# Attention and feed-forward block: single operations on their own slots, a reordered start, strided up-weight rows

## The chip, the cores and the metric

One core of a Trainium2 chip. The metric is the device time of one launch in microseconds (us), lower is better. The core has five engines that each run their own instruction stream in order and meet at semaphores: TensorE (PE, with its weight loads as PEld), VectorE (DVE), ScalarE (ACT), GpSimd (POOL) and SyncE (SP), which here issues nearly all transfers.

## What is computed

x is 16 batches of 128 x 512, the context 16 of 128 x 128. Per batch, with all weights shared:

```
x = x + xattn(layernorm(x), ctx, ctx)      # 16 query heads, 4 key/value heads of 32, rms norm,
                                           # rotary, causal softmax, out @ w_out.T
h = relu(layernorm(x) @ w_up.T + b_up + layernorm(x) @ A_up @ B_up)      # 512 -> 2048
x = x + h @ w_down.T + b_down + h @ A_down @ B_down                      # 2048 -> 512
w_up   = (w_up_q   - 7.5) * repeat(w_up_scale,   64)   # 4-bit values held in int32, 2048 x 512
w_down = (w_down_q - 7.5) * repeat(w_down_scale, 64)   # 512 x 2048
```

The kernel keeps near-float32 accuracy by splitting each fp16 operand into a high and a low part and multiplying three terms (high x high, high x low, low x high).

## The kernel before

**Weights.** The 2048 x 512 up weights and 512 x 2048 down weights arrive as eight groups of 1 MB in a staging ring of three (`load_group`, L269 to L273, SP). A group holds four tiles; there are 32 tiles. A tile is dequantised in place (even tiles on VectorE, L901; odd ones on GpSimd in two steps, L361 and L364), then TensorE adds the low-rank term (L683) and four 128 x 128 transposes (L638) into a 512-column PSUM bank, ScalarE copies out the high half (L500), TensorE subtracts that from the bank with a matmul against minus the identity (`weights_rest`, L698), and ScalarE copies out the low half (L505). Two banks, ff0 and ff1, serve these tiles and the feed-forward of all batches; a bank's next user waits for its last reader.

**Batches.** Each batch runs through: statistics, centring (L514), rotary products, splits of q and k, transposes by DMA (L304, L318), scores (L720), mask and row maximum (L999), exponentials (L543), reciprocal of the sums (L911), normalising on GpSimd (L387), high and low parts of the probabilities (L574, L396), four transposes by DMA (L326), the product with v (L735), its split (L532, L1020), the output projection (L748), residual (L978), second norm and its DMA transpose (L311), four up groups (L767), hidden activations (L930, L605, L939), four down parts (L782) and the result (L1045), which is stored by L277.

**Order.** There is no dynamic scheduler. All engines walk the same counter s (`for s in range(SLOTS)`); each stage has a constant R_... that says at which s batch 0 runs it and at which s batch 1 does, and from there each batch follows PERIOD = 8 slots later. Inside one slot an engine's operations follow the fixed order of its loop body, and each waits on its semaphores in place, so what stands behind a waiting instruction on the same engine waits too. A slot covers many instructions: with 8 slots to a batch, one is about an eighth of a batch's time. On TensorE the scores of a batch stand at slots 11 to 14, the product with v at 20, the projection at 22, up groups at 27 to 30, down parts at 31 to 34 (R_SCORES, R_PV, R_PROJ, R_UP, R_DOWN, L30 to L38). The 32 tiles have slots of their own (TILE_AT, L44); tile and rest are laid down together, and a weight group of the ring is reloaded at the slot of the last tile that frees it. On SP a slot's transposes of k, second norm, q and probabilities come before its weight load (L300 to L331).

**Start.** SP issues batch 0, the two scale tables, the norm weights, weight group 0, six small low-rank loads, batch 1, group 1, w_out, group 2 and more. The quantisation of all scales needs the largest absolute value of seven small arrays (`find_tops`, L837 to L845), a spread over partitions through TensorE (`spread_tops`), and a chain of small operations (`find_scales`), before any tile can be finished. The up bias is loaded as 16 x 128 and transposed on TensorE.

Of the kernel before, what the change touches and what calls it, by code (L numbers as in the profile page):

```python
# [25 lines left out]
PERIOD = 8  # L26
R_STATS, R_CENTRE, R_SINES, R_COSINES, R_ROPE = (0, 1), (1, 2), (1, 3), (1, 4), (2, 6)
R_KSPLIT, R_KLOW = (1, 3), (1, 4)
R_QSPLIT, R_QLOW = (2, 7), (2, 8)
R_SCORES = ((4, 11), (5, 12), (6, 13), (7, 14))  # L30
R_MASK = ((5, 12), (6, 13), (7, 14), (8, 15))
R_EXP = ((6, 13), (7, 14), (8, 15), (9, 16))
R_PROBS = ((7, 14), (8, 15), (9, 16), (10, 17))

R_PSPLIT = ((8, 15), (9, 16), (10, 17), (11, 18))
R_VSUM, R_VSPLIT = (5, 12), (6, 14)
# [7 lines left out]
TILE_AT = tuple(2 + (3 * t) // 4 if t < UP_TILES else 14 + (t - 16) // 2 if t < 26 else t - 7 for t in range(TILES))  # L44
DEQ_LEAD = 4
DVE_TILES = tuple(range(0, TILES, 2))
WOUT_AT = 4
# [3 lines left out]
def build(nc, x, ctx, qw, kw, wo, wuq, wus, bu, wua, wub, wdq, wds, bd, wda, wdb,  # L51
# [12 lines left out]
    SLOTS = PERIOD * (B - 2) + R_RESULT[1] + 1  # L64

    def at(s, r, after=0):
        if s - after == r[0]:
            return 0
        n, rest = divmod(s - after - r[1], PERIOD)
        return n + 1 if rest == 0 and 0 <= n < B - 1 else None  # L70

    with ExitStack() as es:
# [64 lines left out]
        b_nat = sb("b_nat", [HC, P])  # L137
# [23 lines left out]
        ff = [bank("ff0"), bank("ff1")]  # L161
# [3 lines left out]
        vb = bank("vb")  # L165
# [17 lines left out]
        ident_cast, minus_cast, b_turned = sem("ident_cast"), sem("minus_cast"), sem("b_turned")  # L183
# [4 lines left out]
        w_turned, w_high, w_rest, w_low = sem("w_turned"), sem("w_high"), sem("w_rest"), sem("w_low")  # L188
# [20 lines left out]
        wuq_v = wuq.rearrange("(g j p) c -> g p j c", p=P, j=4)  # L209
# [11 lines left out]
        def tiles_at(s):  # L221
            return [t for t in range(TILES) if TILE_AT[t] == s]

        def tiles_to_dequantise(s):
            return [t for t in range(TILES) if max(TILE_AT[4 * (t // 4)] - DEQ_LEAD + t % 4, 1) == s]

# [4 lines left out]
        tile_bank, up_bank, down_bank, up_taken = {}, {}, {}, {}  # L231
        tile_free, up_free, down_free = {}, {}, {}
        freed_by = [None, None]
        taken, last_bank, down_holds = 0, 1, None
        for s in range(SLOTS):
            for t in tiles_at(s):
                last_bank = 1 - down_holds if down_holds is not None else 1 - last_bank
                tile_bank[t], tile_free[t] = last_bank, freed_by[last_bank]
                freed_by[last_bank] = (w_low, t + 1)
            for g in range(4):  # L240
                n = at(s, R_UP, g)
                if n is not None:
                    down_holds = None
                    last_bank = 1 - last_bank
                    up_bank[n, g], up_free[n, g] = last_bank, freed_by[last_bank]
                    taken += 1
                    up_taken[n, g] = taken
                    freed_by[last_bank] = (ff_read, taken)
            n = at(s, R_DOWN)
            if n is not None:  # L250
                last_bank = 1 - last_bank
                down_bank[n], down_free[n] = last_bank, freed_by[last_bank]
                freed_by[last_bank] = (down_read, n + 1)
                down_holds = last_bank
# [4 lines left out]
        def _(sp):  # L259
# [20 lines left out]
            sp.dma_start(s_up[:], wus.rearrange("(c p) b -> p c b", p=P)).then_inc(scales_in, 16)  # L280
            sp.dma_start(s_dn[:], wds.rearrange("(c p) b -> p c b", p=P)).then_inc(scales_in, 16)
# [15 lines left out]
            for s in range(SLOTS):  # L297
                n = at(s, R_KLOW)
# [6 lines left out]
                n = at(s, R_NORM2)  # L305
# [6 lines left out]
                n = at(s, R_QLOW)  # L312
# [6 lines left out]
                for m in range(NN):  # L319
                    n = at(s, R_PSPLIT[m])  # L320
# [6 lines left out]
                for g in range(W_RING, 8):  # L327
                    if TILE_AT[4 * (g - W_RING) + 3] == s:
                        load_group(g)
                n = at(s, R_RESULT)  # L330
                if n is not None:  # L331
                    store(n)
                n = at(s, R_X1, 1)
# [6 lines left out]
        def _(pool):  # L340
# [26 lines left out]
            def keys(n):  # L367
                c, p = n % RING, n % 2
                pool.wait_ge(kv_in[c], 16 * (n // RING + 1))
                kv = kvt[:, c, :]  # L370
                if n > 0:
                    pool.wait_ge(k_low, n)
                pool.tensor_tensor(k_cos[:], kv, cwk[:], ALU.mult).then_inc(k_parts, 1)
# [72 lines left out]
            for s in range(1, SLOTS):  # L446
                probabilities(s)
                cosines(s)
                for t in tiles_to_dequantise(s):
                    if t not in DVE_TILES:  # L450
                        dequant(t)
                n = at(s, R_STATS)
                if n is not None:
                    keys(n)
# [663 lines left out]
```

## Time and profile before

| | |
|---|---|
| median of 3 runs | 587.93 us (584.47 to 588.89) |
| profiled execution, its own time | 587.63 us |
| its span, first to last instruction | 585.8 us |
| mean granted TensorE clock | 0.929 of full |
| busy share PE / DVE / ACT / POOL | 84% / 58% / 54% / 51% |
| chain that ended last: PE, POOL, DMA, issue | 45%, 20%, 10%, 8% |
| first result instruction of batch 0, of batch 15 | 171.76 us, 582.58 us |

### The profile page before, as it was taken

Reading aid. Unit: us, or ns where it says so; the run is one execution under the profiler, and the core shown is the slowest. Engines: PE = TensorE matmul, PEld = TensorE weight load, DVE = VectorE, ACT = ScalarE, POOL = GpSimd, SP = SyncE. Lnnn points to the kernel's source line nnn. Section 1 sums busy time; section 2 is a strip of 40 time slices with the busy share of each in tenths; the row PEclk is TensorE's granted clock in tenths of the full one; section 3 lists DMA queues with packets and bytes.
Section 4 is the critical chain, followed back from the end, with each engine's and each line's share of the span. In section 5 each row is a group of like instructions: output and inputs, shape, how many; then the busy total and the mean of one; then the engine's idle time right before and its main releaser. Section 6 shows DMA issues by size and latency. Waiting matters only on the chain.

```text
span 585.8 us, 12700 instructions
## 1 busy us (share of the span) xinstructions
PE 490.9 (84%) x4744; PEld 343.0 (59%) x4744; DVE 342.3 (58%) x1042; ACT 315.9 (54%) x947; POOL 301.4 (51%) x320
## 2 busy tenths in 40 slices
PE   0267456679888999989999989899999898999997
PEld 0134122337547676667677676767585757586783
DVE  2873513344456777675767758576767676564531
ACT  1557636373565665747484837383847464654210
POOL 3492474483174838383847556556657473625100
PEclk9999555759999999998999999899999998999999
DMA  8930652081053527180817282735455444536010
GB/s 171 284 84 2 191 131 62 29 190 32 10 89 88 123 56 139 39 167 10 167 21 157 39 138 47 131 61 118 56 122 98 84 95 57 103 52 109 2 38 18
DMA packets 144253, 52.87 MB, mean 90 GB/s; under 512 B 132768, under 2 KB 135088, under 8 KB 144144
## 3 DMA queue, kind: packets, MB, share of 16 engines
q1 hardware_dynamic: 141344, 51.56, 43.3%
q10 hardware_dynamic: 2768, 0.34, 0.5%
q8 instruction: 37, 0.61, 0.4%
q14 instruction: 24, 0.20, 0.1%
q0 software_dynamic: 80, 0.16, 0.1%
HBM read 16.39 MB, written 4.19 MB: 35 GB/s over the span
## 4 chain that ended last, share of the span: by engine, by line
PE 45%; POOL 20%; DMA 10%; issue 8%; ACT 6%; DVE 6%; SPq 5%; POOLq 0%; ACTq 0%; DVEq 0%
PE ff L767 19%; PE ff L782 8%; DMA pT<-big 8%; PE tb L748 8%; POOL big L396 6%; POOL pr L387 5%; PE ff L638 3%; SPq L326 3%; POOL y L436 3%; PE tb L735 2%; ACT pr L543 2%; PE sb L720 1%; PE ff L683 1%; POOL inv L379 1%; DVE x L978 1%
## 5 line engine op out<-in xcount | busy, mean ns | idle before, releaser
L767 PE MATMUL ff<-xnT,wu_hi 128*128 128x128 f16 x2048 | 184.2, 223 | 2.7 <-DVE y L1045 1.2
L767 PE MATMUL ff<-xnT,wu_lo 128*128 128x128 f16 x1024 | 180.4, 223 | 0.0
L767 PEld LDWEIGHTS ff<-xnT,wu_hi 128*128 128x128 f16 x2048 | 162.3, 100 | 13.7 <-issue 7.4
L782 PE MATMUL ff<-wd_hi,x 128*128 128x512 f16 x512 | 152.4, 379 | 3.1 <-DVE z L930 2.3
L387 POOL TENSOR_TENSOR pr<-pr,rinv 128x512 f32<-128x512 f32 x64 | 74.5, 1164 | 137.3 <-DVE rinv L911 137.3
L605 ACT ACTIVATE x<-z 128x512 f16<-128x512 f32 x64 | 40.3, 630 | 119.5 <-DVE z L930 119.5
L767 PEld LDWEIGHTS ff<-xnT,wu_lo 128*128 128x128 f16 x1024 | 102.4, 100 | 0.0
L543 ACT ACTIVATE pr<-pr,nmax 128x128 f32<-128x128 f32 x256 | 98.7, 388 | 4.3 <-DVE nmax L999 4.3
L782 PE MATMUL ff<-wd_lo,x 128*128 128x512 f16 x256 | 97.0, 379 | 0.0
L782 PEld LDWEIGHTS ff<-wd_hi,x 128*128 128x128 f16 x512 | 48.8, 98 | 63.4 <-issue 4.9
L396 POOL TENSOR_TENSOR big<-pr,big 128x512 f16<-128x512 f32 x64 | 78.7, 1238 | 3.4 <-ACT big L574 3.4
L930 DVE SCALAR_TENSOR_TENSOR z<-ff,su,b_up 128x512 f32<-128x512 f32 x64 | 47.8, 747 | 46.1 <-PE ff L767 46.1
L999 DVE CUSTOM_DVE_ANT_0 pr<-sb,tabs,score_scale 128x128 f32<-128x128 f32 x256 | 74.2, 346 | 0.0
L939 DVE SCALAR_TENSOR_TENSOR x<-z,x 128x512 f16<-128x512 f32 x64 | 51.8, 809 | 5.0 <-ACT x L605 4.9
L543 ACT ACTIVATION_READ_ACCUMULATOR pr<-pr,nmax 128x1 f32 x256 | 48.2, 188 | 0.0
L574 ACT ACTIVATE big<-pr 128x512 f16<-128x512 f32 x64 | 39.5, 618 | 9.2 <-POOL pr L387 8.9
L782 PEld LDWEIGHTS ff<-wd_lo,x 128*128 128x128 f16 x256 | 25.0, 98 | 30.2
L911 DVE RECIPROCAL rinv<-scaled_sum 128x4 f32<-128x4 f32 x64 | 11.1, 173 | 53.5 <-ACT scaled_sum L548 53.2
L638 PE MATMUL ff<-tabs,big 128*128 128x128 f32 x128 | 30.1, 378 | 8.0 <-POOL big L364 8.0
L426 POOL TENSOR_TENSOR inv<-arg,minus_half 128x1 f32<-128x1 f32 x16 | 9.2, 572 | 50.3 <-DVE arg L985 50.3
L1045 DVE SCALAR_TENSOR_TENSOR y<-ff,sd,y 128x512 f32<-128x512 f32 x16 | 12.0, 751 | 39.3 <-PE ff L782 39.3
L735 PE MATMUL tb<-pT,v 128*32 128x512 f16 x192 | 14.3, 406 | 20.5 <-DMA pT<-big 20.5
(139 smaller groups left out, 716.0 us busy)
## 6 DMA issues: line engine op xcount, KB each, us to landing
xt<-in_x SPq DMA_DIRECT2D x16, 256.0 KB, 3.1
big<-in_L_ffn_w_up_q SPq DMA_DIRECT2D x4, 1024.0 KB, 11.8
big<-in_L_ffn_w_down_q SPq DMA_DIRECT2D x4, 1024.0 KB, 5.4
out<-y SPq DMA_DIRECT2D x16, 256.0 KB, 2.5
kvt<-in_ctx SPq DMA_DIRECT2D x16, 64.0 KB, 3.3
wd_lo<-in_L_xattn_w_out SPq DMA_DIRECT2D x1, 1024.0 KB, 14.1
pT<-big SPq DMA_TRANSPOSE x64, 3.4
wd_hi<-in_L_ffn_w_up_lora_b SPq DMA_DIRECT2D x3, 128.0 KB, 8.6
```

Source lines behind the costliest of these rows:

```text
L387: pool.tensor_tensor(pr[:, m], pr[:, m], rinv[:, p, 4 * m:4 * m + 4].unsqueeze(2).broadcast_to([P, NG, P]), ALU.mult).then_inc(probs, 1)
L396: pool.tensor_tensor(p3[:, m, :, 1, :], pr[:, m], p3[:, m, :, 0, :], ALU.subtract).then_inc(p_low, 1)
L543: last = act.activation(pr[:, m, g, :], pr[:, m, g, :], ACT.Exp, bias=nmax[:, p, j:j + 1], scale=-1.0, accum_out=rsum[:, p, j:j + 1])
L574: act.activation(p3[:, m, :, 0, :], pr[:, m], ACT.Copy).then_inc(p_high, 1)
L605: act.activation(x2_hi[:, HG * g:HG * g + HG, :], z[:, g % 2], ACT.Relu).then_inc(x2_high, 1)
L638: return pe.matmul(dst, src, ident[0:src.shape[0], 0:src.shape[0]], is_transpose=True, **kw)
L748: last = pe.matmul(tb[0][:], a[:, m, :], b[:, m, :], start=(i == 0 and m == 0), stop=(i == 2 and m == NN - 1))
L767: last = pe.matmul(bank[:, P * h:P * h + P], a[:, m, cols], b[:, m, :], start=(h == 0 and m == 0 and i == 0), stop=(m == KC - 1 and i == 2 ...
L782: last = pe.matmul(ff[down_bank[n]][:], a[:, h, :], b[:, h, :], start=(h == 0 and i == 0), stop=(h == HC - 1 and i == 2))
L930: dve.scalar_tensor_tensor(z[:, g % 2], ff[up_bank[n, g]][:].rearrange("p (h t) -> p h t", h=HG), su[:], b_up[:, HG * g:HG * g + HG].unsqu ...
L939: dve.scalar_tensor_tensor(x2_lo[:, HG * g:HG * g + HG, :], z[:, g % 2], 0.0, x2_hi[:, HG * g:HG * g + HG, :], ALU.max, ALU.subtract).then ...
L999: last = dve.tensor_tensor_reduce(pr[:, m, g, :], sbk[m % 2][:, P * g:P * g + P], mask, score_scale[:], 3e38, ALU.add, ALU.min, nmax[:, p, ...
```

## The change

Nothing of the arithmetic changes. What does:

1. **Slots.** PERIOD is 264 and every operation has a slot of its own for batches 0, 1, 2 and 3 (from 3 on, +264 each); tiles, their rests, copies and loads too. The loop bodies keep their fixed order only inside one (now very fine) slot.
2. **Banks.** Four ff banks instead of two. The bank vb goes; the column sum for v is now written into tb[0], the bank of the projection.
3. **Low halves of 15 tiles on VectorE.** For the tiles in LOW_BY_DVE one VectorE subtraction (bank minus high half) replaces TensorE's L698 and ScalarE's L505.
4. **w_out** is reordered on VectorE, not on ScalarE.
5. **Loads.** Up weights: a partition holds four neighbouring rows (8 KB in one piece instead of 4 x 2 KB); the up scales, the down low-rank factor and the up bias follow the same order, the bias in place without a transpose. The down tiles then read every fourth column of the staging buffer, and the up low-rank operand is read with a step of four. SP issues the norm weights first and waits for the five small loads before weight group 0. The up scales go out on ScalarE's queue.
6. **z buffer.** The hidden activations of a group wait for x2_low (VectorE) instead of x2_high (ScalarE) of two groups before.

```
-PERIOD = 8
-R_SCORES = ((4, 11), (5, 12), (6, 13), (7, 14))
-R_PV, R_OSPLIT, R_PROJ, R_X1, R_POW2, R_NORM2 = (13, 20), (14, 21), (14, 22), (15, 23), (15, 23), (16, 24)
-R_UP, R_DOWN = (18, 27), (22, 31)
-R_RESULT = (26, 35)
+PERIOD, FREE = 264, 3
+R_SCORES = ((290, 603, 1007, 1208), (295, 618, 1009, 1209), (349, 636, 1097, 1233), (383, 647, 1130, 1257))
+R_SUMS = ((330, 680, 1078, 1248), (347, 704, 1125, 1324), (368, 746, 1155, 1378), (402, 774, 1181, 1428))
+R_VSUM = (452, 492, 629, 1160)
+R_PV = (504, 903, 1238, 1544)
+R_PROJ = (529, 935, 1374, 1622)
+R_X1 = (570, 929, 1400, 1649)
+R_UP = ((712, 1182, 1498, 1790), (719, 1197, 1508, 1857), (753, 1211, 1518, 1914), (796, 1216, 1613, 1942))
+R_DOWN = ((881, 1228, 1633, 1963), (964, 1378, 1667, 1990), (1114, 1404, 1739, 2016), (1139, 1481, 1741, 2043))
+R_RESULT = (1140, 1487, 1789, 2048)
...
-TILE_AT = tuple(2 + (3 * t) // 4 if t < UP_TILES else 14 + (t - 16) // 2 if t < 26 else t - 7 for t in range(TILES))
+LOW_BY_DVE = (1, 4, 7, 10, 13, 15, 16, 18, 20, 22, 25, 27, 28, 30, 31)
+TURN_AT = (231, 275, 350, 423, 464, 496, 497, 498, 513, 548, 559, 590, 594, 616, 621, 642, 695, 706, 763, 831, 862, 863, 871,
+           904, 925, 955, 979, 984, 1011, 1033, 1045, 1102)
+LOAD_AT = (186, 582, 594, 641, 810)
...
-    def at(s, r, after=0):
-        if s - after == r[0]:
-            return 0
-        n, rest = divmod(s - after - r[1], PERIOD)
-        return n + 1 if rest == 0 and 0 <= n < B - 1 else None
+    def at(s, r):
+        if s in r[0:FREE]:
+            return r.index(s)
+        n, rest = divmod(s - r[FREE], PERIOD)
+        return n + FREE if rest == 0 and 0 <= n < B - FREE else None
...
-        ff = [bank("ff0"), bank("ff1")]
+        ff = [bank("ff0"), bank("ff1"), bank("ff2"), bank("ff3")]
-        vb = bank("vb")
...
-        wuq_v = wuq.rearrange("(g j p) c -> g p j c", p=P, j=4)
+        wuq_v = wuq.rearrange("(g p j) c -> g p j c", p=P, j=4)
...
             load_batch(0)
-            sp.dma_start(s_up[:], wus.rearrange("(c p) b -> p c b", p=P)).then_inc(scales_in, 16)
-            sp.dma_start(s_dn[:], wds.rearrange("(c p) b -> p c b", p=P)).then_inc(scales_in, 16)
             for src, dst in ((kw, kw_bc), (qw, qw_bc)):
...
-            load_group(0)
+            sp.dma_start(s_dn[:], wds.rearrange("(c p) b -> p c b", p=P)).then_inc(scales_in, 16)
             for i in range(3):
...
+            sp.wait_ge(scales_in, 16 * 5)
+            load_group(0)
+            load_group(1)
             load_batch(1)
-            load_group(1)
+            load_group(2)
             sp.dma_start(wo_raw, wo.rearrange("(j p) c -> p j c", p=P)).then_inc(wout_in, 16)
-            load_group(2)
...
                 for i in range(4):
-                    last = turn(bank[:, P * i:P * i + P], stage[:, g % W_RING, i, P * j:P * j + P],
+                    rows = slice(P * j, P * j + P) if t < UP_TILES else slice(j, None, 4)
+                    last = turn(bank[:, P * i:P * i + P], stage[:, g % W_RING, i, rows],
...
-                    pe.matmul(vb[:, 0:1], ones[:], ssq[:, n % 2:n % 2 + 1], start=True, stop=True).then_inc(v_summed, 1)
+                        if projs_before[n] > 0:
+                            pe.wait_ge(x1_ready, projs_before[n])
+                    pe.matmul(tb[0][:, 0:1], ones[:], ssq[:, n % 2:n % 2 + 1], start=True, stop=True).then_inc(v_summed, 1)
...
+            def weights_low(t):
+                dve.wait_ge(w_high, t + 1)
+                hi, lo = ((w[:, t % 4, 512 * (t // 4):512 * (t // 4) + 512] for w in (wu_hi, wu_lo)) if t < UP_TILES else
+                          (w[:, t - UP_TILES, :] for w in (wd_hi, wd_lo)))
+                dve.tensor_tensor(lo, ff[tile_bank[t]][:], hi, ALU.subtract).then_inc(w_low_v, 1)
```

On TensorE the order within one steady period, with the slot in the period, is now: up group 1 (9), projection (38), up group 2 (66), up group 3 (94), column sum for v (104), down part 0 (115), down part 1 (142), scores 0 and 1 of a later batch (152, 153), down part 2 (168), scores 2 (177), down part 3 (195), scores 3 (201), up group 0 of the next batch (206), product with v (224).

## Rows read from the trace of the kernel before

**Rows 1.** Stages: length, busy (x instructions) of PE, PEld, DVE, ACT, POOL; clock, DMA share, GB/s.
```profile
32.20:171.80 139.60, 98.04 (x549) 57.10 (x549) 60.28 (x178) 81.07 (x223) 71.97 (x76) 0.74 0.32 76
32.20:49.20 17.00, 14.74 (x53) 8.65 (x53) 11.45 (x19) 9.52 (x19) 12.04 (x12) 1.00 0.16 31
56.00:110.60 54.60, 29.85 (x104) 15.30 (x105) 18.57 (x64) 26.43 (x80) 28.48 (x32) 0.50 0.41 111
117.40:134.50 17.10, 13.05 (x62) 7.65 (x63) 6.36 (x10) 11.20 (x28) 14.86 (x16) 0.50 0.81 175
171.80:510.80 339.00, 317.06 (x3389) 231.27 (x3390) 233.77 (x730) 202.31 (x647) 199.85 (x205) 0.98 0.49 93
510.80:582.60 71.80, 71.74 (x785) 51.71 (x782) 30.90 (x79) 21.39 (x60) 15.99 (x16) 1.00 0.25 44
```

**Rows 2.** Timeline, VectorE, three of sixteen results: start, duration, instruction, idle before it.
```profile
171.76 0.74 DVE L1045 SCALAR_TENSOR_TENSOR y<-ff,sd,y 128x512 f32<-128x512 f32 x1
510.76 0.75 DVE L1045 SCALAR_TENSOR_TENSOR y<-ff,sd,y 128x512 f32<-128x512 f32 x1 [3.80 <-PE ff L782]
582.58 0.75 DVE L1045 SCALAR_TENSOR_TENSOR y<-ff,sd,y 128x512 f32<-128x512 f32 x1 [8.22 <-PE ff L782]
```

**Rows 3.** Chain that ended last, pieces of one late batch: start, duration, what.
```profile
497.50 2.86 PE tb L748 x12
500.35 10.38 PE ff L782 x48
510.73 2.68 PE ff L767 x48
513.41 0.23 PE sb L720 x4
513.63 0.17 PE vb L706 x2
516.73 0.76 PE tb L735 x12
```

**Rows 4.** Waits, 200 to 480 us: total us, times, longest us.
```profile
PE tb L735 <- DMA pT<-big: 15.9, 10, 2.4
```

**Rows 5.** Timeline of the opening, four instructions of the way to the first tile.
```profile
5.62 0.46 SPq L284 DMA_DIRECT2D wd_hi<-in_L_xattn_q_norm_w  x1
12.14 0.88 DVE L828 TENSOR_REDUCE wmax<-wd_hi 128x1 f32<-128x512 f32 x2 [7.02 <-DMA wd_hi<-in_L_xattn_q_norm_w]
30.73 1.35 POOL L364 TENSOR_TENSOR big<-big,s_up 128x512 f32<-128x512 f32 x1
32.23 1.08 PE L638 MATMUL ff<-tabs,big 128*128 128x128 f32 x4 [1.34 <-POOL big L364]
```

**Rows 6.** Timeline, TensorE: three long idle times while the weights are built.
```profile
69.28 0.61 PE L698 MATMUL ff<-wu_hi,minus 128*128 128x512 f16 x1 [6.01 <-ACT wu_hi L500]
80.06 1.09 PE L638 MATMUL ff<-tabs,big 128*128 128x128 f32 x4 [5.47 <-POOL big L364]
106.63 2.07 PE L748 MATMUL tb<-wo_hi,oT_hi 128*128 128x512 f32 x4 [8.95 <-DVE oT_lo L1020]
```

**Rows 7.** Timeline, SyncE's queue: loads of weight groups and a transpose before one.
```profile
57.32 1.19 SPq L304 DMA_TRANSPOSE kT<-k  x1
58.56 0.58 SPq L273 DMA_DIRECT2D big<-in_L_ffn_w_up_q  x1
99.01 0.57 SPq L273 DMA_DIRECT2D big<-in_L_ffn_w_down_q  x1
```

**Rows 8.** Timeline, VectorE: what waited for the later load.
```profile
104.14 0.69 DVE L901 SCALAR_TENSOR_TENSOR big<-big,s_dn 128x512 f32<-128x512 int32 x1 [8.08 <-DMA big<-in_L_ffn_w_down_q]
```

**Rows 9.** Busy time of line 698 alone while the weights are built (PE, PEld).
```profile
32.20:171.80 139.60, 17.25 (x32) 3.58 (x32) 0.74 0.32 76
```

**Rows 10.** Lines by form, 0 to 172 us: count, busy us, mean ns; idle before.
```profile
L638 PEld LDWEIGHTS ff<-tabs,big 128*128 128x128 f32 x128 | 19.3, 188 | 19.6 <-issue 19.6
L683 PE MATMUL ff<-wd_lo,a_up 48*128 48x512 f16 x16 | 9.2, 576 | 2.1 <-DVE wd_lo L890 2.1
```

More of the change, by code:

```diff
@@ L219, in scale_of, with low_of, wait_lows @@
             return v.unsqueeze(2).broadcast_to([P, 8, QB])
[L221 to L225, printed above, removed]
+        def low_of(t):
+            return (w_low_v, LOW_BY_DVE.index(t) + 1) if t in LOW_BY_DVE else (w_low, t + 1 - len([u for u in LOW_BY_DVE if u < t]))
+        def wait_lows(eng, last):
+            by_dve = len([u for u in LOW_BY_DVE if u <= last])
+            if by_dve <= last:
+                eng.wait_ge(w_low, last + 1 - by_dve)
+            if by_dve:
+                eng.wait_ge(w_low_v, by_dve)
@@ L227, in build @@
         b_pieces = ((b_up3[:, 0:512], b_up_in[:, 0:512], 4), (b_up3[:, 512:], b_up_in[:, 512:], 4),
                     (b_dn3[:], b_dn_in, 5))
[L231 to L234, printed above, removed]
-        for s in range(SLOTS):
[L236 to L239, printed above, removed]
+        tile_bank, up_bank, down_bank, tile_free, up_free, down_free = {}, {}, {}, {}, {}, {}
@@ new lines, in build, with next_bank @@
+        freed_by, last_bank, down_holds = [None] * 4, 3, None
+        def next_bank():
+            b = (last_bank + 1) % 4
+            return (b + 1) % 4 if b == down_holds else b
+        projs_before, sums_before = {}, {}
+        for s in range(SLOTS):
+            n = at(s, R_VSUM)
+            if n is not None:
+                projs_before[n] = len(sums_before)
+            n = at(s, R_PROJ)
+            if n is not None:
+                sums_before[n] = len(projs_before)
+        for s in range(SLOTS):
+            for t in range(TILES):
+                if TURN_AT[t] == s:
+                    last_bank = t % 4 if t < UP_TILES else 2 + t % 2
+                    tile_bank[t], tile_free[t] = last_bank, freed_by[last_bank]
+                    freed_by[last_bank] = low_of(t)
@@ L256, in build @@
+                n = at(s, R_DOWN[g])
+                if n is not None and g == 0:
+                    last_bank = down_holds = 0 if n == 0 else next_bank()
+                    down_bank[n], down_free[n] = last_bank, freed_by[last_bank]
+                    freed_by[last_bank] = (down_read, n + 1)
+                if n is not None and g == 3:
+                    down_holds = None
         block = es.enter_context(nc.Block())
@@ L445, in _ @@
             pool.wait_ge(v_powers_set, 2)
-            for s in range(1, SLOTS):
+            for s in range(SLOTS):
                 probabilities(s)
                 cosines(s)
-                for t in tiles_to_dequantise(s):
-                    if t not in DVE_TILES:
+                for t in range(TILES):
+                    if DEQ_AT[t] == s and t not in DVE_TILES:
                         dequant(t)
-                n = at(s, R_STATS)
+                n = at(s, R_KEYS)
+                if n:
+                    keys(n)
+                n = at(s, R_POW)
                 if n is not None:
-                    keys(n)
+                    norm_factors(n)
                 norm_and_residual(s)
@@ L693, in weights_rest @@
             def weights_rest(t):
-                if t == 0:
+                if t == min(u for u in range(TILES) if u not in LOW_BY_DVE):
                     pe.wait_ge(minus_cast, 1)
@@ L785, in feed_forward @@
                             last.then_inc(down_done, 1)
+            pe.wait_ge(consts_in, 16)
+            spread_tops()
             for s in range(SLOTS):
                 turns(s)
[L789 to L802 removed]
+                for i in range(3):
+                    if LORA_TURN_AT[i] == s:
+                        lora_turn(i)
+                for t in range(TILES):
+                    if REST_AT[t] == s and t not in LOW_BY_DVE:
+                        weights_rest(t)
+                    if TURN_AT[t] == s:
+                        weights(t)
+                for m in range(NN):
+                    if WO_TURN_AT[m] == s:
+                        wout_turn(m)
                 feed_forward(s)
[L804 to L805 removed]
                 products(s)
```

363 lines of the change are left out of this document (197 added, 166 removed).

## The prediction, made before the changed kernel was run

> **What bounds the kernel now.** The stage table comes first, because the busy shares of the whole span mix two stages [rows 1]. From 32.2 to 171.8 us the weights are built: TensorE is busy 98.04 of 139.6 us, and no other engine reaches 82. From 171.8 to 510.8 us only batches run and TensorE is busy 317.06 of 339.0; from 510.8 to 582.6 it has no gap left (71.74 of 71.8). So TensorE is the bound in the second and third stage, and waits are in the first. 
>
> The results of the batches give the rate [rows 2]: 510.76 - 171.76 = 339.0 us for twelve intervals, 28.25 us each. The chain that ended last shows what one batch costs TensorE at the upper level [rows 3]: four up groups of 2.68, the down product 10.38, projection 2.86, product with v 0.76, four scores of 0.23 and the column sum 0.17, together 25.81 us. Twelve are 309.7 us. The other 29.3 us of that stage are 7.4 of longer instructions (317.06 - 309.7, among them those in short stretches of lower clock; the mean is 0.98) and 21.9 of idle time. The waits name it: the product with v waited for the last DMA transpose of the probabilities ten times, 15.9 us, 2.4 at most [rows 4], which makes 19.1 in twelve batches.
>
> **The change, part by part.** I split the profiled execution (587.63 us) into the time to the first result 171.8, twelve intervals 339.0, the last three 71.8, and 5.05 from the last result to the end.
>
> *Opening.* The first tile's transposes began at 32.23, waiting for GpSimd's second multiplication (30.73, 1.35 us) [rows 5]. The norm weights, issued at 5.62, held VectorE until 12.14; now they are issued right behind batch 0, and ScalarE centres batch 0 before its low-rank work, which lets GpSimd's first tiles start earlier. Group 0 is issued later than now, since SP waits for the five small loads, so it becomes the second thing that could be last. The first tile stands at slot 231; if a slot is a tenth of a us (264 of them would be 26.4 us, just over the 25.81 of work) that is 23 us. I take 24, so -8, between 0 (group 0's landing takes back all that was gained) and -9.
>
> *Low halves.* Line 698 cost TensorE 17.25 us for 32 tiles [rows 9]; 15 go: -8.1. VectorE gains 15 subtractions out of PSUM, at the 0.75 us of its nearest form, the result instruction [rows 2], 11 us, beside its 60.28 of 139.6 busy [rows 1]: cost nothing, as that engine has 79 us free; without this cover it would be those 11. Moving w_out's reordering from ScalarE to VectorE, and dropping the bias transpose, I take as nothing for the same reason.
>
> *Idle time in this stage.* It is 139.6 - 98.04 = 41.6 us. Three gaps hold 6.01 + 5.47 + 8.95 = 20.4 of it [rows 6], and I trace all three to weight loads issued late. SP issued the load of group 3 at 58.56, directly behind a transpose of k that itself had to wait (57.32) [rows 7]; a later load went out only at 99.01, VectorE stood 8.08 us in a dequantisation that needed it [rows 8], and the small subtraction that the projection needed was queued behind it on VectorE, so TensorE stood 8.95 us in the projection with finished tiles behind it. In the new order the load of group 3 stands before every transpose of probabilities and of batch 1, and the others right at the tiles that free their buffer; on VectorE the dequantisations stand behind the work of batch 0 that TensorE waits for. With four banks, a tile whose copy is late also no longer stops the next but one. I take the 20.4 as gone and 21.2 as staying; bounds: none goes, or all but 10.
>
> *Clock.* TensorE did 14.74 + 29.85 + 13.05 = 57.6 us of work at its lower level in this stage [rows 1]; at the upper one it would be half. A denser stage should spend less time there, but I can't show how much: between 0 and -25 I take -7, nearer to nothing, as the engine was 87% busy from 32.2 to 49.2 and stayed at the lower level until then.
>
> First result: 171.8 - 8 - 8.1 - 20.4 - 7 = 128.3 us.
>
> *Steady state.* Work stays at 25.81 plus 0.61 of longer instructions. From scores 3 to the product with v there were 6 of 8 slots, 0.75 of 28.25 = 21.2 us; now there are 287 of 264, 1.09 periods or 29 us. Eight us more room against waits of at most 2.4 should end that wait. What is late next is, I think, nothing of that size, but in-order engines always leave something: I take 0.4 of idle time for the 1.83 now, 26.8 us per batch. Bounds: 26.4 (no idle) and 28.25 (all comes back). Twelve: 321.6. The slots of the first results stand 347 and 302 apart, not 264: 121 slots, 0.46 of a period, 12 us, because the attention of batches 1 and 2 was kept back for the weights. I take half, +6, between 0 and 12. The last three stay at 71.8 and the end at 5.05.
>
> Sum: 128.3 + 6 + 321.6 + 71.8 + 5.05 = 532.7, **533 us**. The profiled execution stands 0.3 us under the median of 587.93, which I leave out.
>
> **The strides.** The 64 transposes of down tiles now load every fourth column of a float32 buffer, and the up low-rank operand is read with a step of four. No row shows TensorE reading with a step. The nearest are the plain forms, 188 ns for a float32 weight load and 576 ns for the low-rank matmul [rows 10]. If either took twice as long, it would be 64 x 0.188 = 12.0 and 16 x 0.576 = 9.2 us; below nothing there is no reason for a gain. I take 0, since the loads run beside other matmuls, and carry 21 us as a rival.
> The Trainium skill, "SBUF — State Buffer", section "Door 1: The DMA port swizzle", speaks against this part: accesses that stay within a 16-byte line run at full bandwidth and each one that crosses to a new line pays, so that a step of four float32 is at the edge. By that rule the down tiles would pay (an estimate by it, with the row's 188 ns: 545 us) and the fp16 operand, with a step of 8 bytes, would not. No row of this trace can say.
>
> **The rivals.**
> - *The steady waits come back* at another place: 12 x (28.25 - 26.8) = 17.4 more, 550 us. For it: four engines above 50% busy in one fixed order. Against: only one place waits now. 0.12.
> - *The weight stage keeps its 27 us* of idle time and low clock, since group loads and dequantisation are what they were: 533 + 27.4 = 560. For it: the load ring is still three groups. Against: the late issues are visible in rows. 0.12.
> - *The strides cost*: 533 + 21 = 554. 0.08.
> - *Slower: the shared bank.* The column sum for v now goes into tb[0], so TensorE stops there (slot 104) until VectorE's residual of the same batch (65) has read it, with all four down parts queued behind. That residual stands behind the reciprocal of sums 2 (58), which waits for ScalarE's exponentials (56). A late exponential thus stops TensorE, which it can't do now. Slack by the slots: 39 of 264, 4 us. It would turn the sign from (587.6 - 532.7) / 12 = 4.6 us of standstill per batch; with 6 it gives 533 + 72 = 605. 0.07.
> - *Nothing gained*: the waits of both stages all re-form and pay for the shorter opening, 588 us. 0.05.
>
> My forecast has 0.56. The range takes in its bounds and the three milder rivals: low, first result 117 (all but 10 us of the idle time gone, clock as taken), no delay of the first intervals, 26.5 per batch, 117 + 318 + 71.8 + 5.05 = 512, I say 513; high, first result 150, 12 us of delay, 28.25 per batch, 578, I say 576. Within 1% is what a measurement of this kernel can't tell from no change. Faster by over 1%: forecast and first three rivals, 0.88; within 1%: 0.05; slower: 0.07.
>
> **What would show it.** First transposes of a tile at 23 to 26 us; no VectorE wait for a down load above 3 us; first result near 128; thereafter 26.4 to 27.3 us between results, with no wait of the product with v for its transpose; the column sum with no idle time before it (or, if the rival holds, some us in each batch, released by VectorE's residual); float32 weight loads of down tiles at 188 ns. The forecast is wrong if the first result comes after 150, or if intervals stay over 28.

## The result

The changed kernel takes 516.28 us (median of four, 516.16 to 516.8) against 587.44 beside it: ratio 0.8796, 95% interval 0.8761 to 0.8831, 12% faster. The same kernel in a later comparison gave 516.6 against 588.83, 0.8785 (0.8759 to 0.881). The profiled execution took 516.16 us, with a span of 514.4.

The page of the changed kernel, its first lines, the granted clock and the chain that ended last:

```profile
span 514.4 us, 12676 instructions
...
PE 471.2 (92%) x4728; PEld 335.4 (65%) x4728; DVE 353.7 (69%) x1061; ACT 302.4 (59%) x928; POOL 293.0 (57%) x320
...
PEclk9996797899999999999999999999999999999999
...
PE 83%; DVE 5%; DMA 4%; POOL 2%; SPq 2%; issue 2%; ACT 1%; POOLq 0%
```

The chain is TensorE for 83% (45% before) and GpSimd for 2% (20% before). The stages, in the columns of [rows 1]:

```profile
27.40:125.30 97.90, 84.41 (x536) 54.30 (x536) 69.54 (x195) 70.68 (x198) 64.02 (x67) 0.86 0.42 105
27.40:38.00 10.60, 9.71 (x44) 6.49 (x44) 9.79 (x44) 8.69 (x36) 7.94 (x10) 1.00 0.23 50
...
41.40:58.50 17.10, 13.78 (x54) 7.59 (x53) 12.18 (x18) 11.22 (x21) 12.99 (x13) 0.50 0.50 118
...
75.60:82.40 6.80, 5.14 (x49) 5.14 (x50) 0.18 (x1) 6.00 (x25) 5.33 (x6) 0.50 0.16 32
...
96.10:99.50 3.40, 3.21 (x10) 1.60 (x11) 2.82 (x6) 2.44 (x5) 1.45 (x3) 0.51 1.14 295
...
155.10:440.20 285.10, 285.10 (x3110) 207.74 (x3107) 213.48 (x677) 183.30 (x600) 174.19 (x187) 1.00 0.54 100
440.20:511.10 70.90, 70.87 (x771) 50.89 (x768) 28.15 (x60) 17.04 (x41) 13.84 (x14) 1.00 0.15 35
```

The row to look at is 155.10 to 440.20: TensorE is busy 285.10 of 285.10 us, so it waits for no other engine and no transfer, at a granted clock of 1.00.
```profile
125.28 0.75 DVE L1133 SCALAR_TENSOR_TENSOR y<-ff,sd,y 128x512 f32<-128x512 f32 x1 [0.97 <-PE ff L861]
```
```profile
440.18 0.75 DVE L1133 SCALAR_TENSOR_TENSOR y<-ff,sd,y 128x512 f32<-128x512 f32 x1 [2.33 <-PE ff L861]
```
```profile
511.11 0.75 DVE L1133 SCALAR_TENSOR_TENSOR y<-ff,sd,y 128x512 f32<-128x512 f32 x1 [8.22 <-PE ff L861]
```

Split as the prediction split it, in us of the two profiled executions:

| | before | forecast | after | gained |
|---|---|---|---|---|
| to the first result | 171.8 | 128.3 | 125.3 | 46.5 |
| twelve intervals | 339.0 | 327.6 | 314.9 | 24.1 |
| last three | 71.8 | 71.8 | 70.9 | 0.9 |
| to the end | 5.05 | 5.05 | 5.05 | 0 |
| sum | 587.6 | 532.7 | 516.2 | 71.5 |

### The profile page after: what moved, and what is told of

The parts are those of the page before. It is cut to its first block, busy times and chain, and to the rows that moved or that the text cites. A ratio compares the mean times of both kernels' runs of the same rounds, so it can differ in the third digit from the quotient of the medians.

```text
span 514.4 us, 12676 instructions
## 1 busy us (share of the span) xinstructions
PE 471.2 (92%) x4728; PEld 335.4 (65%) x4728; DVE 353.7 (69%) x1061; ACT 302.4 (59%) x928; POOL 293.0 (57%) x320
## 4 chain that ended last, share of the span: by engine, by line
PE 83%; DVE 5%; DMA 4%; POOL 2%; SPq 2%; issue 2%; ACT 1%; POOLq 0%
PE ff L846 32%; PE ff L861 30%; PE tb L826 8%; PE ff L710 4%; PE sb L799 2%; PE tb L814 2%; PE ff L757 2%; DMA wd_hi<-in_L_xattn_q_norm_w 1%; SPq L395 1%; DMA xnT<-xn_parts 1%; DVE big L977 1%; POOL big L469 1%; DMA qT<-q 1%; ACT pr L616 1%; DVE wd_lo L966 1%
## 5 line engine op out<-in xcount | busy, mean ns | idle before, releaser
L846 PE MATMUL ff<-xnT,wu_hi 128*128 128x128 f16 x2048 | 178.9, 221 | 3.8 <-DMA xnT<-xn_parts 2.9
L846 PE MATMUL ff<-xnT,wu_lo 128*128 128x128 f16 x1024 | 176.0, 220 | 0.0
L846 PEld LDWEIGHTS ff<-xnT,wu_hi 128*128 128x128 f16 x2048 | 158.1, 99 | 13.4 <-issue 9.7
L460 POOL TENSOR_TENSOR pr<-pr,rinv 128x512 f32<-128x512 f32 x64 | 68.3, 1070 | 61.1 <-DVE rinv L999 61.0
L846 PEld LDWEIGHTS ff<-xnT,wu_lo 128*128 128x128 f16 x1024 | 101.0, 99 | 0.0
L1027 DVE SCALAR_TENSOR_TENSOR x<-z,x 128x512 f16<-128x512 f32 x64 | 56.9, 891 | 0.7 <-ACT x L678 0.6
L492 POOL TENSOR_TENSOR t_cos<-xc,cw 128x512 f32<-128x512 f32 x16 | 25.8, 1611 | 18.4 <-ACT xc L587 18.3
L605 ACT ACTIVATE oT_hi<-tb,v_scales 128x512 fp32r<-128x512 f32 x16 | 11.0, 688 | 40.5 <-PE tb L814 40.5
L710 PE MATMUL ff<-tabs,big 128*128 128x128 f32 x128 | 27.0, 343 | 0.2 <-DVE big L977 0.2
L799 PEld LDWEIGHTS sb<-kT,qT 96*128 96x128 f16 x256 | 18.7, 101 | 10.9 <-DVE nmax L1087 1.1
```

Source lines behind the costliest of these rows:

```text
L460: pool.tensor_tensor(pr[:, m], pr[:, m], rinv[:, p, 4 * m:4 * m + 4].unsqueeze(2).broadcast_to([P, NG, P]), ALU.mult).then_inc(probs, 1)
L710: return pe.matmul(dst, src, ident[0:src.shape[0], 0:src.shape[0]], is_transpose=True, **kw)
L846: last = pe.matmul(bank[:, P * h:P * h + P], a[:, m, cols], b[:, m, :], start=(h == 0 and m == 0 and i == 0), stop=(m == KC - 1 and i == 2 ...
L1027: dve.scalar_tensor_tensor(x2_lo[:, HG * g:HG * g + HG, :], z[:, g % 2], 0.0, x2_hi[:, HG * g:HG * g + HG, :], ALU.max, ALU.subtract).then ...
```

## The experiments

Two theories stand against each other. **Waits**: the 71 us are standstills of in-order engines that the new places of the operations take away. **Work**: part of it is cheaper work and transfers (low halves off TensorE, wider pieces of the weight loads, the held-back start). The runs that change one place of the order test the first, the others the second.

### One number for one operation: the product with v 60 slots earlier

```
-R_PV = (504, 903, 1238, 1544)
+R_PV = (504, 903, 1238, 1484)
```

> The changed kernel with the product with v 60 slots earlier from batch 3 on (1484 instead of 1544; it moves in front of the last two down parts and two score groups of the batch before), nothing else. The room from the last scores to it falls from 287 to 227 of 264 slots, from 28 to 22 us; the kernel before had 21.2. Theory 'room': the wait for the transpose is back, 1 to 4 us in each of 12 batches, intervals of 27 to 30 us instead of 25.9, 530 to 560 us. Rival 'the fine order shortened the way of the probabilities itself': no wait and 516 to 518.

588.74 us, ratio 1.0005 (0.9975 to 1.0036): 72 us more than the changed kernel, by the place of one group of twelve matmuls from batch 3 on. The wait came back, as expected; the price is far above the expected 530 to 560 us, which counted only the wait itself. The first result, then the waits of this run from 200 to 480 us, then a stage of it:

```profile
126.48 0.75 DVE L1133 SCALAR_TENSOR_TENSOR y<-ff,sd,y 128x512 f32<-128x512 f32 x1 [0.99 <-PE ff L861]
```

```profile
PE tb L814 <- DMA pT<-big: 34.1, 9, 4.1
```

```profile
250.80:254.20 3.40, 3.40 (x18) 1.06 (x11) 0.00 (x0) 3.26 (x10) 1.23 (x2) 0.50 0.00 0
254.20:281.50 27.30, 24.05 (x266) 18.04 (x263) 18.62 (x60) 12.61 (x43) 14.52 (x16) 1.00 0.51 95
281.50:284.90 3.40, 2.92 (x16) 0.88 (x17) 0.19 (x3) 3.37 (x13) 1.04 (x1) 0.50 0.02 5
```

TensorE waits 34.1 us in nine batches, 3.8 each, for the probabilities' last transpose, more than twice what it was before the change [rows 4]. Most intervals are 31.4 us, which is also above the 28.25 of the kernel before: the first result keeps its gain of 45 us, and the steady stage loses more than the change had given it. And the clock falls: 3.4 us at 0.50 (6.8 in four of twelve batches), 27.3 us at 1.00, and again. In the changed kernel it doesn't fall in the 415 us from 99.5 to the end. So a wait costs more than its length: 3.8 us of waiting and some 1.7 us for each stretch at 0.50 (3.4 us of work at half rate) make the 5.5 us by which most intervals grew.

The timelines also show that the way of the probabilities did not get shorter. From the last scores of a batch (on TensorE, L720 before, L799 after) to the last of four transposes on SyncE's queue, before and after:

```profile
325.67 0.39 PE L720 MATMUL sb<-kT,qT 96*128 96x128 f16 x4
```
```profile
341.76 2.76 SPq L326 DMA_TRANSPOSE pT<-big  x2
```
```profile
258.63 0.39 PE L799 MATMUL sb<-kT,qT 96*128 96x128 f16 x4
```
```profile
278.56 2.61 SPq L395 DMA_TRANSPOSE pT<-big  x2
```
```profile
287.53 0.83 PE L814 MATMUL tb<-pT,v 128*32 128x512 f16 x12
```

Both rows of the queue hold the last two transposes. From the scores' row to the end of the issue it is 18.9 us before and 22.5 after; what changed is that the product with v comes 28.9 us after the scores' row. The other batches of the two traces agree (18.7 to 19.6 us and 22.5 to 22.8). The wait ended because its consumer was put later, not because the work in front of it became faster.

### The same move in the coarse order

Three kernels were made from the one before. The first moves the product with v and what follows up to the second norm, the last one moves the feed-forward and the result too:

```
-... = (13, 20), (14, 21), (14, 22), (15, 23), (15, 23), (16, 24)      # b6, b7 and b8
+... = (13, 21), (14, 22), (14, 23), (15, 24), (15, 24), (16, 25)
-R_UP, R_DOWN = (18, 27), (22, 31)                                     # b8 only
+R_UP, R_DOWN = (18, 28), (22, 32)
-R_RESULT = (26, 35)
+R_RESULT = (26, 36)
```

> The kernel before with the product with v, its split, the projection, the residual and the second norm one slot of eight later from batch 1 on. Theory 'room': the wait for the last transpose of the probabilities (1.6 us per batch) goes, intervals fall from 28.25 to 26.4 to 26.9, 12 x 1.5 = 16 to 20 us less, 568 to 572. Rival 'another wait takes its place': the up groups now follow the second norm's transpose by two slots instead of three and TensorE waits there; intervals stay above 27.5 and the time above 580.

620.22 us, ratio 1.0533 (1.0484 to 1.0583). The rival is right: the wait for the probabilities is gone, and this one stands in its place (waits from 200 to 480 us), with intervals of 30.4:

```profile
PE ff L767 <- DMA xnT<-xn_parts: 29.7, 10, 3.8
```

> The kernel before with everything from the product with v to the result one slot later from batch 1 on, so that only the room between the probabilities' last transpose and the product with v grows (6 to 7 of 8 slots) and the distance from the second norm to the up groups stays. Theory 'two rooms are needed': both waits are absent, intervals of 26.0 to 26.8 us instead of 28.25, 12 x 1.7 = 20 us less, 565 to 573. Rival 'the coarse order itself costs': the wait appears in a third place and intervals stay above 27.5, 580 or more.

580.49 us, ratio 0.9865 (0.9828 to 0.9902): the rival's time, but not by a wait in a third place. Intervals fall from 28.25 to 27.5, and the old wait is smaller but there:

```profile
PE tb L735 <- DMA pT<-big: 12.1, 10, 2.3
```

With a whole slot more room the way of the probabilities itself, measured as above, took 20.1 to 21.6 us to the end of its last transpose instead of 18.7 to 19.6, presumably since VectorE, ScalarE and GpSimd now have other work at the same slots. A slot of eight is 3.5 us; the waits to be removed are 1.6. I found no whole-slot move that fits, and that is what single slots repair; that none exists isn't shown.

> Both moves in the kernel before. If the two places are independent, the gains add: 548 to 560 us. What then is left to the changed kernel's 516 is the opening (5 us), the low halves (4 to 8), the clock and the finer order. Rival: one gain hides the other and the sum falls short by more than 5 us.

614.06 us, ratio 1.0437 (1.0393 to 1.0481): b6's move plus the one below, and nowhere near the expected 548 to 560. It is 6 us under b6's move alone, about the 5 us that the one below gains alone, so the two places do add, on top of a wrong move.

### Weight loads

```
             for s in range(SLOTS):                     # SyncE's loop of the kernel before
+                for g in range(W_RING, 8):
+                    if TILE_AT[4 * (g - W_RING) + 3] == s:
+                        load_group(g)
                 n = at(s, R_KLOW)
...
-                for g in range(W_RING, 8):
-                    if TILE_AT[4 * (g - W_RING) + 3] == s:
-                        load_group(g)
```

> The kernel before with one move: in each slot SyncE issues the weight group's load ahead of the slot's transposes. Theory 'loads stuck behind transposes' (the idle-time step of the prediction): group 3 goes out at about 46 us instead of 58.56 and group 5 some us before 99, the waits of 6.0, 5.5 and 9.0 us on TensorE shrink: 10 to 20 us less, 568 to 578. Rival 'the engines' order is the trouble, not the queue': GpSimd and VectorE stand in other waits at the same places and the time falls by less than 4 us.

582.95 us, ratio 0.9896 (0.9847 to 0.9944); first result at 164.8 instead of 171.8. SyncE's queue, and TensorE's longest wait:

```profile
40.53 0.39 SPq L273 DMA_DIRECT2D big<-in_L_ffn_w_up_q  x1
```
```profile
91.10 1.19 SPq L307 DMA_TRANSPOSE kT<-k  x1
92.34 0.57 SPq L273 DMA_DIRECT2D big<-in_L_ffn_w_down_q  x1
```
```profile
100.08 1.22 PE L748 MATMUL tb<-wo_hi,oT_hi 128*128 128x512 f32 x2 [9.07 <-DVE oT_lo L1020]
```

Between the theory and the rival: 5.3 us by the medians, 7 by the first result. Group 3 goes out 18 us earlier; the gap of 6.0 us is gone, the one of 5.5 is 3.2. The load of group 5 also went out 11 us earlier (71.01 instead of 82.38), behind these gaps. The later load, that of group 6 and not of group 5 as expected above, is as late as before, now behind a transpose of an earlier slot (91.10), 9 us after the last tile that frees its buffer (that tile began at 81.3), and the wait of 9.07 us stays with it. So the prediction's cause holds for group 3; for the later load this kernel did not remove it, and whether an earlier load alone would end the 9 us stays open.

```
-LOAD_AT = (186, 582, 594, 641, 810)
+LOAD_AT = (495, 582, 594, 641, 810)
```

> The changed kernel with one number altered: SyncE issues weight group 3 behind the four transposes of batch 0's probabilities (slot 495 instead of 186), so at about 49 us instead of 37.45. Theory 'late loads stop in-order engines': the data lands near 55, VectorE stands in the dequantisation of tile 12 meanwhile with the low half of tile 4 behind it, which frees the bank of tile 8, so TensorE stands 4 to 7 us around 50 to 57: 520 to 524 us, first result 4 to 8 us later. Rival 'the load has slack': group 3 is turned only at 65, 16 us after 49, and the time stays within 1 us of 516.3.

518.12 us (514.86 to 519.11), ratio 0.8798 (0.8745 to 0.8852): not to be told from the changed kernel. The load did go out late:

```profile
50.44 0.57 SPq L342 DMA_DIRECT2D big<-in_L_ffn_w_up_q  x1
```

It was 37.45. The first half of the expected chain came: VectorE stood in the dequantisation of tile 12 until 56.25 for this load. The second didn't:

```profile
56.25 0.69 DVE L977 SCALAR_TENSOR_TENSOR big<-big,s_up 128x512 f32<-128x512 int32 x1 [3.92 <-DMA big<-in_L_ffn_w_up_q]
```

VectorE had stood 2.5 us three operations later in the changed kernel too, for ScalarE's high half of tile 7, so most of the 3.92 replaced that, and TensorE lost 0.20 us there. Tile 12 began at 65.0 in the changed kernel, well behind 56. The late wait found work in front of it that was late anyway: slack, here.

### Low halves

```
-LOW_BY_DVE = (1, 4, 7, 10, 13, 15, 16, 18, 20, 22, 25, 27, 28, 30, 31)
+LOW_BY_DVE = (1, 25, 28)
```

with slots for the 12 tiles' matmul and copy between their high half and the bank's next user.

> The changed kernel with the low halves of 12 of the 15 tiles given back to TensorE (matmul against minus the identity) and ScalarE; tiles 1, 25 and 28 stay on VectorE. Theory 'TensorE is the bound while the weights are built': 12 more matmuls of 0.22 to 0.54 us on TensorE and 12 copies of 0.59 on ScalarE, plus the hops between them: 4 to 8 us more, 520 to 524. Rival 'there was room': TensorE still stands 13.5 us in that stage and they fall into it, 516 to 517.

544.46 us, ratio 0.9257 (0.9204 to 0.931): 28 us more, first result at 151.1. The direction is that of the first theory, the size three and a half to seven times what it gave. Its stage, and the longest of its stretches at 0.50, which last 17.1, 27.3, 10.2 and 10.2 us here against 17.1, 6.8 and 3.4 above:

```profile
27.50:151.10 123.60, 99.84 (x549) 60.00 (x548) 64.75 (x183) 77.93 (x215) 67.23 (x67) 0.74 0.34 83
...
65.60:92.90 27.30, 23.10 (x110) 14.89 (x111) 10.31 (x45) 14.23 (x41) 14.57 (x18) 0.50 0.39 111
```

TensorE is busy 15.4 us longer (99.84 against 84.41) and stands 10.3 us longer (23.8 against 13.5). Twelve matmuls at 0.6 us are 7.2 us at most; the rest of the busy time goes, I think, with the low clock. The low half on TensorE is a round trip, ScalarE to TensorE to ScalarE, in front of the bank's next user, and one subtraction on VectorE is not. A reservation: the twelve slots were mine, put into an order laid out without them; a new layout for them might cost less than 28.

### Strided reads

```
-rows = slice(P * j, P * j + P) if t < UP_TILES else slice(j, None, 4)
+rows = slice(P * j, P * j + P)
-..., b_up3[:, 512 * g:512 * g + 512].rearrange("k (p i) -> k i p", i=4)
+..., b_up3[:, 512 * g:512 * g + 512]
```

> The changed kernel with plain reads: TensorE's transposes of down tiles read 128 neighbouring columns instead of every fourth, and the up low-rank operand is read without a step. This mixes up the order of the hidden units between the two weight matrices, so the products belong to other rows; nothing else changes, and every instruction stays in its place. Theory 'the step costs': in the changed kernel's trace the low-rank matmul of an up tile takes 607 ns at the granted clock 1.0 where the plain one of a down tile takes 386, and a float32 weight load of a down tile 196 to 220 ns where that of an up tile takes 140. Some nine up tiles and all down tiles lie at the upper clock, TensorE is nearly always busy there, so 9 x 0.22 + 16 x 0.09 = 3.4 us go: 513 us, with 386 ns and 140 ns in the rows. Rival 'the step is hidden': 516.3, with the same rows or with the time turned into waits.

516.53 us (515.32 to 517.87), ratio 0.8786 (0.8748 to 0.8825): no difference. But the prices are real. Lines by form where the clock is at 1.00: the changed kernel's up tiles (59 to 71 us; weight loads of the transposes and low-rank matmuls) and its down tiles (84 to 125; of this 3.4 us are at 0.50, and from 99.6 on alone the mean is 209 ns too), then the down tiles with plain reads (84 to 100):

```profile
L710 PEld LDWEIGHTS ff<-tabs,big 128*128 128x128 f32 x28 | 2.9, 141 | 3.1 <-issue 3.1
...
L757 PE MATMUL ff<-wd_lo,a_up 48*128 48x512 f16 x7 | 4.2, 607 | 0.0
```
```profile
L710 PEld LDWEIGHTS ff<-tabs,big 128*128 128x128 f32 x56 | 8.0, 209 | 3.4 <-issue 3.4
```
```profile
L710 PEld LDWEIGHTS ff<-tabs,big 128*128 128x128 f32 x20 | 2.1, 140 | 1.1 <-issue 1.1
```

A float32 weight load takes 209 ns with a step of 16 bytes and 140 without; the fp16 operand takes 607 ns with a step of 8 bytes, and in the plain run 387. The 3.4 us that this is worth on TensorE did not reach the end; with plain reads the stretches of low clock lay elsewhere (6.8 us twice). The Trainium skill, "SBUF — State Buffer", section "Door 1: The DMA port swizzle", has every access that crosses to a new 16-byte line pay, and steps within a line free: this trace agrees for the float32 load (209 ns against 140) and not for the fp16 operand, whose step of 8 bytes should be free by it (607 ns against 387).

### The held-back start

```
-            sp.wait_ge(scales_in, 16 * 5)
             load_group(0)
```

> The changed kernel without SyncE's wait for the five small loads ahead of weight group 0. Theory 'the hold pays': group 0 goes out at about 7.1 us instead of 11.07, shares the transfer engines with the scales and the bias, these land 2 to 3 us later, the search for the largest values starts that much later and so does the first tile: 518 to 519 us. Rival 'order is enough': the small loads are all issued by 3.4 us, well ahead of 7.1, so the norm weights and scales land as now (the reductions start at 11.9 +- 0.5) and the time stays at 516.3 or falls by at most 1, since group 0 is not what the first tile waits for.

517.47 us (514.65 to 519.42), ratio 0.8798 (0.8751 to 0.8845): nothing. The search for the largest values began at 12.38 us instead of 11.91 and the first tile's transposes at 27.8 instead of 27.4. The hold neither pays nor costs that can be seen; the small loads are ahead of group 0 in the queue in both kernels.

### The clock of the first stage

```
+            def warm(k, bank=ff[3]):
+                for _ in range(k):
+                    pe.matmul(bank[:], ident16[:], ident16[:].unsqueeze(1).broadcast_to([P, 4, P]), ...)
+            warm(22)                 # ahead of the largest values; 26 behind, 9 behind the low-rank transposes
...
+                    pe.wait_ge(row_max, 3)           # e10 only: third and fourth transposes of w_out
+                    warm(12 if m == 2 else 4, sbk[0])
...
+                        warm(9, sbk[0])              # e10 only: ahead of the column sum of batch 0
...
+                                pe.wait_ge(row_max, 7)
+                                warm(13, sbk[0])     # e10 only: ahead of up group 0 of batch 0
```

> The changed kernel again, unaltered, as the base for what runs beside it on the same chip. Both theories: 514.5 to 519 us; the spread of the small experiments before (514.7 to 519.4) is then that of the kernel itself, and differences below 2 us between them say nothing.

516.6 us (516.4 to 517.22), the base of the next two. Its first result comes at 126.23 us. From 27.4 us on its trace has two stretches at 0.50 on record, of 6.8 and 3.4 us; before the first change on record, at 56, its float32 transposes take 1.12 us for four, so it was at the lower level there as well.

> The changed kernel with 57 matmuls of no use (identity by identity, 128 x 512 fp16, into a bank that is free until its first tile) in TensorE's idle times of the opening: 22 before the search for the largest values, 26 behind it, 9 behind the low-rank transposes. Theory 'the clock costs': TensorE is at 2.4 GHz when the first tile comes at 27.4 us instead of 38.0; 9.7 us of work up to 38 run at twice the rate, but the softmax of batch 0 on ScalarE and VectorE sets the end there, so 2 to 5 us less. Rival 'TensorE's clock in the opening is covered': within 1 us of the base, or slower by up to 3 if the extra matmuls come in the way of the small ones.

519.68 us (519.22 to 520.73), ratio 0.8838 (0.8812 to 0.8864), 3 us slower than its base, so the rival, at its worse end. The clock was at 1.00 from 9.9 us, but the way to the first tile is VectorE's and its transposes began 0.4 us earlier only; then the clock fell at 30.4 and again at 40.6, where TensorE stands. Up to 78 us the two traces agree within 0.3. The first results lie 2.2 us apart (128.41 and 126.23), and the product with v of batch 1 shows where that begins, here and in the base:

```profile
103.23 0.83 PE L814 MATMUL tb<-pT,v 128*32 128x512 f16 x12 [3.12 <-DMA pT<-big]
```
```profile
102.64 0.83 PE L814 MATMUL tb<-pT,v 128*32 128x512 f16 x12 [0.20 <-DMA pT<-big]
```

TensorE is there 2.3 us earlier than in the base, stands 3.12 us for the last transpose, and starts 0.6 us later; the other 1.6 us come behind it, where a stretch at 0.50 lies at 105.5 to 108.9, and in the base in front of it (97.0 to 100.4). Why the transpose came later no run shows.

> As the kernel with 57 matmuls of no use, and 38 more where TensorE waits while the weights are built: 12 and 4 ahead of the third and fourth transposes of w_out, 9 ahead of the column sum of batch 0, 13 ahead of up group 0 of batch 0, into the score bank that is free there. Theory 'idle gaps take the clock down and the low clock prolongs the stage': the stretches at 0.5 (41.4 to 58.5, 75.6 to 82.4, 96.1 to 99.5, 27.3 us with 22.1 us of work in them) shrink or go, up to 11 us less together with the opening, first result at 114 to 120, 505 to 512 us. Rival 'other engines hold the stage': the clock rises and the time stays within 2 us of the base.

511.07 us (509.48 to 513.13), ratio 0.8691 (0.8664 to 0.8717) against the base's 0.8785 (0.8759 to 0.881): 5.5 us faster than the changed kernel and 8.6 faster than with the opening's matmuls alone, the fastest of all. TensorE, then the stage:

```profile
36.82 2.75 PE L874 MATMUL sb<-ident 128*128 128x512 f16 x12
```
```profile
27.40:120.80 93.40, 83.10 (x574) 50.85 (x573) 71.99 (x194) 70.39 (x197) 66.20 (x67) 0.96 0.46 110
32.60:36.00 3.40, 3.40 (x16) 2.27 (x16) 3.14 (x22) 3.34 (x19) 1.62 (x2) 0.50 0.01 2
36.00:97.40 61.40, 54.36 (x428) 33.67 (x427) 47.43 (x100) 45.91 (x120) 50.79 (x49) 1.00 0.59 145
97.40:100.90 3.50, 3.50 (x12) 2.44 (x12) 3.02 (x7) 3.09 (x8) 1.70 (x3) 0.51 0.61 119
```

The stretches at 0.50 after 27.4 us shrink from the 27.3 us on record in the changed kernel's first trace to 6.8, and the first result comes at 120.9 instead of 126.2. The first theory had the mechanism right, the price about half: it allowed 11 us and 5.5 came, because in these stretches ScalarE and VectorE are as busy as TensorE (11.22 and 12.18 of 17.10 us against 13.78) and then hold the stage, I think.

## Why the prediction was right, step by step

The time lies in the range and faster was right; the forecast of 533 was 17 us too high. The steps hold in kind, with one reservation: that late loads caused the idle time is shown for a part of it only. These are the terms.

*Opening*, 8 us forecast, 4.8 measured (32.23 to 27.44). The changed kernel, four instructions of the way:

```profile
11.07 0.82 SPq L342 DMA_DIRECT2D big<-in_L_ffn_w_up_q  x2
...
15.98 0.62 POOL L430 TENSOR_SCALAR big<-big 128x512 f32<-128x512 int32 x1 [0.34 <-DMA big<-in_L_ffn_w_up_q]
...
26.66 0.61 PE L757 MATMUL ff<-wd_lo,a_up 48*128 48x512 f16 x1 [2.13 <-DVE wd_lo L966]
...
27.44 0.90 PE L710 MATMUL ff<-tabs,big 128*128 128x128 f32 x3 [0.17 <-DVE big L977]
```

Group 0 was not last: its data were in at 15.98. The norm weights came 3.4 us earlier and this went through, but VectorE's own chain of small operations, and its low-rank subtraction that the first tile's low-rank matmul waits for, now set the first tile.

*Low halves and clock*, 8.1 and 7 forecast: TensorE's busy time from the first tile to the first result fell by 13.6 us (98.04 to 84.41), 15.1 by the sum. Work done at the lower level fell from 57.6 us to 31.8 (9.71 + 13.78 + 5.14 + 3.21 in the stages above), which at half rate is 12.9 us, nearly twice my 7. This and the 8.1 overlap, as low halves that left had been done at the lower level, and the strided reads took some back. That the low halves are worth more than their matmuls, I had not seen: experiment, 28 us for twelve.

*Idle time*, 41.6 us, 21.2 forecast to stay; 13.5 stayed. The gap of 8.95 us in the projection is gone, those that are left are 2.9 and less. Two of the longest:

```profile
41.13 0.88 PE L710 MATMUL tb<-tabs,x 128*128 128x128 f32 x4 [2.91 <-DVE wo_lo L971]
```
```profile
77.26 0.40 PE L846 MATMUL ff<-xnT,wu_hi 128*128 128x128 f16 x2 [2.93 <-DMA xnT<-xn_parts]
```

The direction and the places were right. That the late loads were the cause is shown for group 3 only (7 us of 12 for its two gaps).

*Steady state*, 26.8 forecast, 25.91 measured. Here two sub-terms were mis-sized. I left 0.4 us of idle time and there is none. And I kept 0.61 us per batch of "longer instructions" as if they were work: most of it was the stretches of low clock (three of 3.4 us at half rate are 5.1 of the 7.4 us), and these went with the waits; 0.1 stayed. Twelve times 0.89 are 10.7 of the 17 us. 25.81 from [rows 3] was the number to trust. The first intervals cost 4.0 us more than 25.9, 6 forecast; the last three 70.9, 71.8 forecast.

*Strides*, 0 forecast with 21 as the rival: the operations do cost more (1.5 and 1.6 times), the kernel doesn't.

*Rivals.* The shared bank never stopped TensorE: between 155.1 and 440.2 us there is no idle time at all ahead of anything, the column sum included, so its 4 us of slack by the slots were enough. That waits come back at another place did not happen, but the two moved kernels show that it easily does: 28.25 became 30.4 by the move that ended the wait I had named.

Of the 71 us, then, the two traces place 46 before the first result and 24 in the twelve intervals. The experiments price parts of the new order, not shares of the 71: the low halves of twelve tiles are worth 28 us in it, and the place of one consumer 72, which is three times what the steady stage had gained, because the misplaced product makes the intervals longer than they were before the change. Such prices overlap and don't add up to a budget. Not tried alone are the early norm weights, the wider pieces of the weight loads, w_out on VectorE, the new wait for the z buffer and the four banks; as for the banks, in the new order the low half of a tile stands behind the turns of later tiles, so I expect two to lock it.

## What to carry to other kernels

When engines run in order and one of them is nearly full, read for each of its waits two numbers: how long the way of the data is, and how far behind its producer the consumer stands; put the consumer past the end of the way (here 28.9 us behind its producer for a way of 22.5), and check the next consumer down the line, because the wait moves there (one group 60 of 264 slots too early cost 72 us, one slot of eight too late cost 32). Count time above an engine's bare work as waiting until shown otherwise, its slower clock included. Slots of 3.5 us could not remove waits of 1.6 here; single ones of 0.1 us did.

## What the runs showed of the hardware

- The granted clock also falls where TensorE's waits are short. With 3.8 us of standstill per batch of 31 us it is at 0.50 for 3.4 or 6.8 us in nearly every batch; with 1.6 us per batch of 28 us three times in 339 us; in the changed kernel, with 1.3 us from 99.5 to 125.3, 2.8 us to 155.1 and none after that, never.
- From 41.4 to 58.5 us it stayed at 0.50 with TensorE 81% busy, 7.30 of its 13.78 busy us in float32 transposes. Why it didn't rise sooner no run shows. With matmuls of no use in the idle times (2.75 us of them from 36.82 on, two groups more up to 46, and one ahead of up group 0) it stayed at 1.00 from 36.0 to 97.4.
- A moving fp16 operand read with a step of 8 bytes takes 607 ns for 512 columns at either clock. A plain one takes 387 at the upper clock and 604 at the lower (the latter in the kernel before, 56 to 110 us): at the lower clock the step costs next to nothing, at the upper it does.
